# Wide cross attention of a decoder kernel: the output projection in four quarters (steps 0, 2, 4, 6) in place of two halves (steps 2, 4)

## What is computed

```python
k_new = concat([keys @ Wk.T + bk, key_grid @ Wgk.T + bgk])     # 512 keys
v_new = concat([values @ Wv.T + bv, key_grid @ Wgv.T + bgv])
q = queries @ Wq.T + bq
att = softmax(where(mask, -inf, q k / sqrt(64)) over all 512 keys)
x = x + (att @ v_new) @ Wo.T + bo                              # queries = layernorm(x)
```

## Time and profile before

| what | before |
|---|---|
| median of 3 runs | 4368.42 us |
| the profiled execution, its own time | 4378.19 us |
| its span, first to last instruction | 4376.5 us |
| mean granted TensorE clock | 0.922 |
| the phase of the change | from about 2597 us to 3668 us of the span |

### The profile page before, as it was taken

One profiled execution on the slowest core, in us unless ns is written; L12 is line 12 of the kernel. 1 busy time (PEld: TensorE's weight loads), 2 busy tenths in 40 slices (PEclk: granted clock), 3 DMA queues, 4 the chain that ended last, 5 costly groups with the idle time before them and its releaser, 6 DMA issues. The chain is left out here.

```text
span 4376.5 us, 98035 instructions
## 1 busy us (share of the span) xinstructions
PE 3843.4 (88%) x33384; PEld 3130.3 (72%) x33384; DVE 2647.1 (60%) x6223; ACT 1940.9 (44%) x4006; POOL 2208.3 (50%) x2418
## 2 busy tenths in 40 slices
PE   6999699976489999899699978999999997599991
PEld 5887577754368888789577856766666675499991
DVE  4665366648974444566456537676676676855553
ACT  2554255544223333233144436666666663255550
POOL 2333222212236666677554416676676673266665
PEclk9999699976799999999799979999999997599996
DMA  1000000000249999899200014433434431365554
GB/s 54 0 0 1 28 13 10 5 21 24 92 150 331 326 328 327 275 319 319 78 1 0 0 60 105 106 88 101 103 88 103 103 87 36 121 220 216 216 195 122
DMA packets 286519, 522.09 MB, mean 119 GB/s; under 512 B 36192, under 2 KB 134624, under 8 KB 275296
## 3 DMA queue, kind: packets, MB, share of 16 engines
q1 hardware_dynamic: 153312, 338.68, 22.5%
q0 software_dynamic: 104192, 127.99, 11.6%
q10 hardware_dynamic: 28800, 52.44, 3.1%
HBM read 370.08 MB, written 132.12 MB: 115 GB/s over the span
## 5 line engine op out<-in xcount | busy, mean ns | idle before, releaser
L563 POOL TENSOR_TENSOR L_xattn_p<-L_xattn_p,L_xattn_rsum 128x1024 f32<-128x1024 f32 x256 | 484.1, 1891 | 229.4 <-DVE L_xattn_rsum L665 225.6
L2081 POOL DMA_INDIRECT L_ffn_xin<-zs,L_ffn_listed x400 | 446.3, 1116 | 243.9 <-issue 112.8
L2469 POOL DMA_INDIRECT L_ffn_back<-ys,L_ffn_slots x320 | 314.2, 982 | 133.0 <-issue 64.9
L1304 ACT ACTIVATE L_attn_pT<-L_attn_bank 128x384 f32<-128x384 f32 x512 | 223.4, 488 | 324.7 <-PE L_attn_bank L1410 178.7
L600 DVE TENSOR_REDUCE L_xattn_negmax<-L_xattn_scores 128x2 f32<-128x1024 f32 x256 | 310.4, 1212 | 82.2 <-PE L_xattn_scores L772 82.2
L699 ACT ACTIVATE L_xattn_p<-L_xattn_scores,L_xattn_negmax 128x512 f32<-128x512 f32 x512 | 346.4, 687 | 4.5 <-DVE L_xattn_negmax L600 3.7
L784 PE MATMUL L_xattn_turned<-ident,L_xattn_p 128*128 128x128 f32 x2048 | 272.2, 277 | 41.0 <-POOL L_xattn_p L563 41.0
L2113 PE MATMUL L_ffn_bank<-L_ffn_xT,L_ffn_w 128*128 128x256 f32 (+1 forms) x1536 | 306.4, 346 | 0.0
L1194 DVE TENSOR_REDUCE L_attn_negmax<-L_attn_bank 128x1 f32<-128x128 f32 x512 | 146.4, 286 | 211.0 <-PE L_attn_bank L1410 209.9
L784 PEld LDWEIGHTS L_xattn_turned<-ident,L_xattn_p 128*128 128x128 f32 x2048 | 232.2, 142 | 55.5 <-POOL L_xattn_p L563 49.5
L2086 POOL TENSOR_TENSOR L_ffn_w<-L_ffn_w,L_ffn_w 128x2048 fp32r<-128x2048 f32 x40 | 185.6, 4641 | 170.7 <-ACT L_ffn_w L2210 170.7
(11 more groups left out here) (401 smaller groups left out, 11312.5 us busy)
## 6 DMA issues: line engine op xcount, KB each, us to landing
L_ffn_w<-in_L_ffn_w SPq DMA_DIRECT2D x80, 1024.0 KB, 5.2
L_ffn_w<-in_L_ffn_w SPq DMA_DIRECT2D x192, 384.0 KB, 5.4
ys<-L_ffn_yo ACTq DMA_DIRECT2D x200, 256.0 KB, 4.8
kv<-kv_v_row SPq DMA_DIRECT2D x128, 256.0 KB, 4.1
L_xattn_mask<-in_L_xattn_mask POOLq DMA_DIRECT2D x256, 128.0 KB, 2.5
L_xattn_k_raw<-kv SPq DMA_DIRECT2D x128, 256.0 KB, 2.6
L_xattn_v<-kv SPq DMA_DIRECT2D x16, 2048.0 KB, 10.3
kv<-kv_k_row SPq DMA_DIRECT2D x96, 256.0 KB, 4.3
```

What stands on the lines that cost most here:

```text
L563: pool.tensor_tensor(p[:, s % 4, :, :], p[:, s % 4, :, :], rsum[:, s % 2, :, None].to_broadcast([P, 2, c.keys]), ALU.mult).then_inc(n_read ...
L1304: act.activation(pT[:, h, 0:WIDTH], t_ps[SLOT[2 * g + i]][:, 0:WIDTH], ACT.Exp, scale=c.scale).then_inc(t_taken, 1)
L2081: pool.indirect_dma_start(xin[j % U][:, t, :], None, zs, bass.IndirectOffsetOnAxis(ap=listed[:, 2 * at + t:2 * at + t + 1], axis=0)).then_ ...
L2469: pool.indirect_dma_start(back[:, i % NG, :], None, ys, bass.IndirectOffsetOnAxis(ap=slots[:, tile, k:k + 1], axis=0)).then_inc(b_in[i % N ...
```

## The change

OUT leaves AT_STEP and gets a table of its own: four quarters of 12 matmuls (rows 0 to 127 with pairs 0 to 3 in step 0, with pairs 4 to 7 in step 2, rows 128 to 255 likewise in steps 4 and 6), each issued after the turning and before what AT_STEP names. One bank now holds OUT from step 0 to step 6, so O0 and O1 both go to the other one, and the numbers of uses per bank are 8 and 6 in place of 7 and 7. VectorE's `add_output` moves from step 4 to step 6. No instruction is added or left out beyond that.

```diff
-        AT_STEP = {1: O7, 2: OUT, 3: O0, 5: O1, 6: Z, 7: O2, 8: Q0, ...
+        AT_STEP = {1: O7, 3: O0, 5: O1, 6: Z, 7: O2, 8: Q0, ...
+        OUT_STEPS = {0: (0, 0), 2: (0, 4), 4: (1, 0), 6: (1, 4)}
+        IN_BANK = ((O7, O0, O1, Z, Q0, Q1, Q2, Q3), (OUT, O2, O3, O4, O5, O6))
+        BANK = {use: k for k in range(2) for use in IN_BANK[k]}
...
         def made(b, use):
-            return (b + 1) * 7 + use // 2 + 1
+            uses = IN_BANK[BANK[use]]
+            return (b + 1) * len(uses) + uses.index(use) + 1
...
                         if s == 4:
                             normalise(b + 1)
+                        if s == 6:
                             add_output(b)
...
-                def output_rows(t, u, step):
-                    for g in range(PAIRS):
-                        if t == 0 and g == PAIRS - 1:
-                            pe.wait_ge(a_free[O7 % 2], emptied(step, O7))
+                def output_rows(step, u, t, first):
...
+                    if (t, first) == (0, 0):
...
+                        pe.wait_ge(a_free[BANK[OUT]], emptied(step, OUT) - 1)
+                    for g in range(first, first + 4):
+                        if g == PAIRS - 1:
+                            pe.wait_ge(a_free[BANK[O7]], emptied(step, O7))
...
+                    if (t, first) == (1, 4):
+                        e.then_inc(a_ready[BANK[OUT]], 1)
...
                         turn(*later(b, s, -1))
+                        if s in OUT_STEPS:
+                            output_rows(b, u, *OUT_STEPS[s])
                         if s in AT_STEP:
                             use_bank(b, AT_STEP[s], u)
-                        if s == 4 and exists(b + of(OUT)):
-                            output_rows(1, u, b).then_inc(a_ready[OUT % 2], 1)
```

More of the change, by code:

```diff
@@ L456, in wide_attention_phase @@
         O7, OUT, O0, O1, Z, O2, Q0, O3, Q1, O4, Q2, O5, Q3, O6 = range(14)
-        AT_STEP = {1: O7, 2: OUT, 3: O0, 5: O1, 6: Z, 7: O2, 8: Q0, 9: O3, 10: Q1, 11: O4, 12: Q2, 13: O5, 14: Q3, 15: O6}
+        AT_STEP = {1: O7, 3: O0, 5: O1, 6: Z, 7: O2, 8: Q0, 9: O3, 10: Q1, 11: O4, 12: Q2, 13: O5, 14: Q3, 15: O6}
+        OUT_STEPS = {0: (0, 0), 2: (0, 4), 4: (1, 0), 6: (1, 4)}
+        IN_BANK = ((O7, O0, O1, Z, Q0, Q1, Q2, Q3), (OUT, O2, O3, O4, O5, O6))
+        BANK = {use: k for k in range(2) for use in IN_BANK[k]}
         PAIR_OF = {O0: 0, O1: 1, O2: 2, O3: 3, O4: 4, O5: 5, O6: 6, O7: 7}
@@ L467, in made @@
         def made(b, use):
-            return (b + 1) * 7 + use // 2 + 1
+            uses = IN_BANK[BANK[use]]
+            return (b + 1) * len(uses) + uses.index(use) + 1
         def emptied(b, use):
-            return (b + 1) * 7 + use // 2 + 2
+            return made(b, use) + 1
         def exists(b):
@@ L607, in a_bank @@
                 def a_bank(b, use):
-                    dve.wait_ge(a_ready[use % 2], made(b, use))
+                    dve.wait_ge(a_ready[BANK[use]], made(b, use))
                     if exists(b + of(use)):
-                        return a_ps[use % 2]
-                    dve.sem_inc(a_free[use % 2], 1)
+                        return a_ps[BANK[use]]
+                    dve.sem_inc(a_free[BANK[use]], 1)
                 def rest_of_queries(b, use):
@@ L622, in rest_of_queries @@
                             e = dve.scalar_tensor_tensor(qT[1][:, g, :], rows[:, j * S:(j + 1) * S], bqs[:, g:g + 1], qT[0][:, g, :].bitcast(F32), ALU.add, ALU.subtract)
-                        e.then_inc(a_free[use % 2], 1)
+                        e.then_inc(a_free[BANK[use]], 1)
                 def rest_of_rows(b):
@@ L629, in rest_of_rows @@
                     if rows is not None:
-                        dve.tensor_tensor(zT[1][:, :, :], rows[:, :].rearrange("p (g q) -> p g q", q=S), zT[0][:, :, :].bitcast(F32), ALU.subtract).then_inc(a_free[Z % 2], 1)
+                        dve.tensor_tensor(zT[1][:, :, :], rows[:, :].rearrange("p (g q) -> p g q", q=S), zT[0][:, :, :].bitcast(F32), ALU.subtract).then_inc(a_free[BANK[Z]], 1)
                 def rest_of_values(b, use, u):
@@ L637, in rest_of_values @@
                         slot = y_slot(use, u)
-                        dve.tensor_tensor(yT[1][:, slot, :], rows[:, 0:S], yT[0][:, slot, :].bitcast(F32), ALU.subtract).then_inc(a_free[use % 2], 1)
+                        dve.tensor_tensor(yT[1][:, slot, :], rows[:, 0:S], yT[0][:, slot, :].bitcast(F32), ALU.subtract).then_inc(a_free[BANK[use]], 1)
                 def rest_of_keys(b, g):
@@ L658, in add_output @@
                         done = b + of(OUT)
-                        dve.tensor_tensor(tile_pair(x_res, done), rows[:, :].rearrange("p (t d) -> p t d", d=D), tile_pair(x_res, done), ALU.add).then_inc(a_free[OUT % 2], 1)
+                        dve.tensor_tensor(tile_pair(x_res, done), rows[:, :].rearrange("p (t d) -> p t d", d=D), tile_pair(x_res, done), ALU.add).then_inc(a_free[BANK[OUT]], 1)
                 def body(b, u):
@@ L711, in round_out @@
                         return
-                    act.wait_ge(a_ready[use % 2], made(b, use))
-                    rows = a_ps[use % 2]
+                    act.wait_ge(a_ready[BANK[use]], made(b, use))
+                    rows = a_ps[BANK[use]]
                     if use == Z:
@@ L735, in body @@
                         copy_turned(*later(b, s, -1))
-                        if s in AT_STEP and AT_STEP[s] != OUT:
+                        if s in AT_STEP:
                             round_out(b, AT_STEP[s], u)
@@ L762, in scores @@
                         q = (Q0, Q1, Q2, Q3)[g // 2]
-                        pe.wait_ge(a_free[q % 2], emptied(b - 1, q))
+                        pe.wait_ge(a_free[BANK[q]], emptied(b - 1, q))
                     if not (isinstance(n, int) and n < 2):
@@ L785, in turn @@
                         e.then_inc(t_ready[i], 1)
-                def output_rows(t, u, step):
-                    for g in range(PAIRS):
-                        if t == 0 and g == PAIRS - 1:
-                            pe.wait_ge(a_free[O7 % 2], emptied(step, O7))
+                def output_rows(step, u, t, first):
+                    b = step + of(OUT)
+                    if not exists(b):
+                        if (t, first) == (0, 0):
+                            pe.wait_ge(a_free[BANK[OUT]], emptied(step, OUT) - 1)
+                            pe.sem_inc(a_ready[BANK[OUT]], 1)
+                        return
+                    if (t, first) == (0, 0):
+                        if isinstance(b, int) and b == 0:
+                            pe.wait_ge(w_split, 2)
+                        pe.wait_ge(a_free[BANK[OUT]], emptied(step, OUT) - 1)
+                    for g in range(first, first + 4):
+                        if g == PAIRS - 1:
+                            pe.wait_ge(a_free[BANK[O7]], emptied(step, O7))
                         slot = g if g else 8 * (1 - u)
                         for y_piece, w_piece in PIECES:
-                            e = pe.matmul(a_ps[OUT % 2][:, t * D:(t + 1) * D], yT[y_piece][:, slot, t * P:(t + 1) * P], wo[w_piece][:, g, :],
+                            e = pe.matmul(a_ps[BANK[OUT]][:, t * D:(t + 1) * D], yT[y_piece][:, slot, t * P:(t + 1) * P], wo[w_piece][:, g, :],
                                           start=g == 0 and y_piece == 1, stop=g == PAIRS - 1 and y_piece + w_piece == 0, skip_group_check=True)
-                    return e
+                    if (t, first) == (1, 4):
+                        e.then_inc(a_ready[BANK[OUT]], 1)
                 def use_bank(step, use, u):
                     b = step + of(use)
-                    k = use % 2
+                    k = BANK[use]
                     if not exists(b):
@@ L810, in use_bank @@
                     if use in QUERIES:
-                        pe.wait_ge(a_free[Z % 2], emptied(step, Z))
+                        pe.wait_ge(a_free[BANK[Z]], emptied(step, Z))
                     if use in PAIR_OF:
@@ L816, in use_bank @@
                         pe.wait_ge(v_in[u], b // 2 * 16 + 16 if isinstance(b, int) else (b - u) * 8 + 16)
-                    if use == OUT and isinstance(b, int) and b == 0:
-                        pe.wait_ge(w_split, 2)
                     pe.wait_ge(a_free[k], emptied(step, use) - 1)
@@ L830, in use_bank @@
                                                   start=cc == 0 and w_piece == 1, stop=cc == DC - 1 and w_piece + z_piece == 0, skip_group_check=True)
-                    elif use == OUT:
-                        output_rows(0, u, step)
-                        return
                     else:
```

## The result

The changed kernel takes 4424.6 us (median of 4 runs, 4423.58 to 4428.27), the kernel before 4366.2 us (4 runs, 4362.96 to 4369.81): the ratio is 1.0135, with a 95% interval of 1.0117 to 1.0153. It is 58 us slower; the forecast was 52 us (4420 against 4368.4). The profiled execution of the changed kernel took 4428.27 us, its span is 4426.7 us, its mean granted clock 0.917.

The account below looks back on a forecast made before the run. TensorE was taken to bound the phase (191.35 of 200 us busy), so only gaps and clock could change: -10.4 + 39.1 - 0.7 (tail) + 23.8 = +51.8 us on 4368.4, giving 4420 us; range 4386 to 4438.

Parts of the forecast that it names:

- Quarter into step 0: 12 projection matmuls moved from step 2 to step 0 wait for nothing and cover gap A whole: -10.4 us.
- gap A: TensorE's wait in step 1 before turn(0), until GpSimd has normalised: 1.15 us in 9 sequences, forecast to go.
- GpSimd's chain holds no projection matmul: The 16.33 us from T to turn(4) hang on O7, VectorE and DMAs; moving projection matmuls leaves them nearly unchanged.
- T: End of O7 in step 1, where the next scores start, about 3154.76 in the timeline; start of GpSimd's chain.
- Rival 4: Step 3's mask load, issued sooner, gets ahead of the values and lands in 2.5 us: 4340 us; faster, chance 0.06.
- Gap B: TensorE's wait in step 5 before turn(4), sequences 1 to 14: grows by 2.8 us to 4.3 us, +39.1 us.
- Banks, Z, `add_output`, the reciprocal: 0: Quarter and `add_output` in step 6: O2's bank free in time, Z not delayed, earlier reciprocal gains nothing; each 0.
- Clock: Half clock (1.2 GHz) after all 14 gaps B, 2.1 us each, less 5.9 us already lost: +23.8 us.
- The rival in which the clock holds: Gap B grows but no half clock follows: +28 us, 4396 us; chance 0.13.
- The transposes: Eight transposes come first after gap B; if they bring no full clock, each gap costs the larger loss: about 4428 us.
- The gaps after the loop's jump: 0: Waits at step 0 ahead of the scores in six sequences, 2.51 us the longest; nothing fills them, nothing won.
- DMA arbitration: By round-robin between queues, a 128 KB load beside a 2048 KB one would be hardly held up; trace: 6.1 against 2.5 us.

## Why the prediction was right

- **TensorE sets the phase's time.** Right: the gaps and the clock explain the whole of the 59.2 us. The four terms of the sum came out within 2 us each; nearly all of what is missing between 51.8 and 59.2 us lies in a place that I had put at nothing, the loop's jump.
- **Quarter into step 0.** Right: gap A gone in nine sequences, -10.3 us against -10.4, and no wait before the quarter.
- **GpSimd's chain holds no projection matmul.** Right, and the step on which the result hangs: 16.34 us from T to turn(4) after 16.33. That it is a drain behind a slow mask load was argued before the runs and is now shown by two of them, one that takes the drain away and one that makes the load land in 2.4 us. What I had not seen is that the landing follows the values and not the mask's own issue. Rival 4, in which a sooner issue gets ahead of the values, did not come: the issue was 0.42 us sooner, still 4.6 us behind that of the values.
- **Gap B.** Right, +38.7 us against +39.1, but so close by luck: two terms were each off by 0.2 us a gap and made up for each other. The mask load was issued 0.42 us sooner after T (3183.70 - 3177.30 = 6.40 against 6.82), but landed 6.5 us after that and not 6.1; so it landed no sooner, where I took 0.2 us. For the same reason the waits before the power are 91.4 us and not 86, which I had named as a sign. And a quarter shifts the next scores by 3173.33 - 3171.74 = 1.59 us, not by half of 2.99, so that the work beside the chain fell by 2.79 us and not by 2.99.
- **Banks, Z, `add_output`, the reciprocal: 0.** Right: alone they give a ratio of 1.0007, with an interval that holds no change, and the changed kernel shows no wait before the first quarter, Z or O2.
- **Clock.** Right for the gaps B: +23.8 was forecast and some +23 us measured. All 14 gaps lost clock, as I took it, each 1.4 to 3.0 us, with a mean of 2.2 against 2.1. Its baseline was partly luck: the 5.9 us that I subtracted for losses already there came in one profile of the kernel before and not in the other. Nor does the length of a gap alone tell: 1.78 us was followed by half clock in sequence 10 before, while 2.51 us after a jump and 2.88 us in the kernel with the first half cut were not. The rival in which the clock holds fell, and the kernel with matmuls in the gap shows it from the other side.
- **The transposes.** Both sizes of loss came again: sequence 8 lost 0.7 us in the turning and ended earlier, sequence 7 lost 0.9, then 1.7 in O1 and 0.35 in the scores. By the rule of Part 4 (PE-mode transpose) of the Trainium skill's page "TensorE: Matmul & The Clock Gate", that transposes don't bring the full clock, every gap was to pay the larger loss of 2.6 us. The trace does not bear that out: five of the 14 lost only 1.4 to 1.6 us. The total by it, 4428 us, is not far enough from 4424.6 us to decide.
- **The gaps after the loop's jump: 0.** Wrong by some 11 us; I had said only that a quarter would not fill them, not that they could grow. The gaps grew by 4.9 us, and half clock followed all six in the changed kernel (9.4 us of loss) where it had followed two (3.5 us). It is the largest single miss. The longer gaps go with a second fetch of instructions, as said above; that this is their cause is not shown by an edit.
- **DMA arbitration.** From the turn-taking between queues that the Trainium skill's page "DMA: Bandwidth & Descriptors" (Queues, rings and completion order) states, I had concluded that the small load would be hardly held up beside the large one. The trace disagrees with my conclusion, though not with the turn-taking: 6.5 us beside the values, 2.4 us without. In the kernel before, the mask load of step 2 was issued at 3158.42 and landed after 8.0 us. The first row is of 3157 to 3162.3 us, the others of 3162.3 to 3167.5 us (packets, MB, share):

```profile
q1 hardware_dynamic: 647, 1.33, 76.1%
...
q1 hardware_dynamic: 653, 1.27, 71.8%
q0 software_dynamic: 544, 0.26, 27.1%
```

  Until 3162.3 us no packet of a mask moves (q0), only those of SyncE's loads (q1); after that both loads of masks, 272 packets each, go in between the others. So the delay lies before their first packet. Why they begin so late is open.

## What to carry to other kernels

A wait that the profile shows before one engine may be set by a chain that never touches the work you move: measure from the last common point to the wait, and see what of your work lies beside it. Here cover was moved from a 16 us chain that needed it to a 1 us gap, at an exchange of 39 for 10; the clock and the longer gaps after the jump added 31. The chain itself was the cheaper target: a drain that orders two small instructions of one engine also waits for the DMAs that this engine has issued, and a semaphore on the one instruction does not. And where a chain hangs on a small load, look for the large load that it lands with: moving the large one gave 100 us (4424.6 to 4324.9), issuing the small one 0.4 us sooner gave nothing.

## What the runs showed of the hardware

- After GpSimd's drain the next instruction started 0.78 to 0.80 us after the landing of GpSimd's last load, in sequences 1 to 14 of every profile with the drain, at landings of 2.4 to 7.5 us alike; with a semaphore it started 0.29 us after the add.
- A 128 KB load landed after 2.4 us without, and after 5.6 to 7.5 us beside, a 2048 KB load that another queue had been given 4.5 to 5.0 us before; it landed mostly some 1.0 us behind that one. Issued 0.42 us sooner, it landed at the same time.
- Where one half is cut, the gaps of a mean 2.75 and 2.87 us were followed by 1.2 GHz in 12 of 14 sequences each, those of 3.75 to 4.79 us in 14 of 14. Useless matmuls in the gap made the kernel 46 us faster than leaving it idle.
- Writing out a loop of 7 turns took away six gaps of 1.9 to 3.6 us at the jump. With the loop, a 16 KB instruction fetch had started just before each; where two had started in the last microsecond, the gap was 3.4 to 3.8 us.
